# Second attention layer: keys projected for four batches at a time, and the even step's exponentials taken head by head from the score bank

## What is computed

```python
q = (layernorm(x) @ Wq)                # 16 heads of 64
k, v = ctx[:, :77] @ Wk, ctx[:, :77] @ Wv            # 77 text keys
k_ip, v_ip = ctx[:, 77:] @ Wk_ip, ctx[:, 77:] @ Wv_ip   # 51 image keys
out = softmax(q k^T / 8) v + softmax(q k_ip^T / 8) v_ip
x = x + out @ Wo + bo
```

## Time and profile before

| | |
|---|---|
| median of 3 runs | 666.91 us (665.79 to 667.15) |
| profiled execution | 667.46 us, of which the span of instructions is 665.7 us |
| PE busy | 617.7 us (93%) |
| DVE busy | 492.1 us (74%) |
| ACT busy | 461.8 us (69%) |
| POOL busy | 309.8 us (47%) |
| chain that ended last | PE 64%, ACT 11%, issue 9%, POOL 7%, DVE 4%, DMA 3% |

### The profile page before, as it was taken

The page is one execution under the profiler, slowest core; times in us unless marked ns, Lnnn a source line. Parts: engine busy times, 40 slices in busy tenths (PEclk is TensorE's granted clock), DMA queues, the critical chain, the costliest instruction groups (busy, mean ns, idle before and its releaser), DMA issues.

```text
span 665.7 us, 16842 instructions
## 1 busy us (share of the span) xinstructions
PE 617.7 (93%) x5833; PEld 568.2 (85%) x5833; DVE 492.1 (74%) x1370; ACT 461.8 (69%) x1397; POOL 309.8 (47%) x444
## 2 busy tenths in 40 slices
PE   5898999999999999999999999999999987998990
PEld 5787888898888899999989989889888976988990
DVE  6578676586886869888898896888675675674654
ACT  5988999998888986656565656665663545665762
POOL 4365354354434444444444352445336575565550
PEclk9999999999999999999999999999897999998995
DMA  9800000000000000346654060000000001212215
GB/s 226 256 2 1 1 2 1 2 1 3 1 1 1 3 17 2 127 95 126 114 118 91 2 159 1 2 1 1 1 6 28 26 25 47 64 57 65 77 49 198
DMA packets 49612, 33.36 MB, mean 50 GB/s; under 512 B 9508, under 2 KB 46088, under 8 KB 49528
## 3 DMA queue, kind: packets, MB, share of 16 engines
q1 hardware_dynamic: 47256, 27.61, 16.8%
q0 software_dynamic: 2272, 4.67, 2.1%
HBM read 17.64 MB, written 14.63 MB: 48 GB/s over the span
## 4 chain that ended last, share of the span: by engine, by line
PE 64%; ACT 11%; issue 9%; POOL 7%; DVE 4%; DMA 3%; SPq 0%; POOLq 0%; DVEq 0%; ACTq 0%
PE ps_h L812 7%; PE ps_j L590 7%; PE ps_s L759 7%; ACT scores L987 7%; PE ps_t L797 6%; PE ps_h L829 6%; PE ps_j L369 5%; PE ps_j L371 4%; PE ps_j L370 4%; PE ph L1717 4%; PE py L1728 4%; POOL probs L1531 3%; POOL xs_scratch L1642 2%; PE pf L620 2%; PE pf L677 1%
## 5 line engine op out<-in xcount | busy, mean ns | idle before, releaser
L1531 POOL TENSOR_TENSOR probs<-scores,rsums 128x308 f32<-128x308 f32 (+1 forms) x192 | 153.5, 814 | 203.5 <-DVE rsums L1276 203.3
L987 ACT ACTIVATE scores<-scores,neg_max 128x128 f32<-128x128 f32 x256 | 99.8, 398 | 0.1
L956 ACT ACTIVATE probsT<-ps_t 128x512 f32<-128x512 f32 x128 | 76.3, 596 | 20.2 <-PE ps_t L797 19.8
L797 PE MATMUL ps_t<-ident,probs 128*128 128x128 f32 x512 | 78.4, 276 | 7.9 <-ACT probsT L956 4.3
L759 PE MATMUL ps_s<-KT,QT 64*128 64x128 f32 x1024 | 75.7, 288 | 0.8 <-ACT KT L859 0.8
L853 ACT ACTIVATE QT<-ps_j 128x512 f32<-128x512 f32 x64 | 38.1, 596 | 52.4 <-PE ps_j L371 52.4
L812 PE MATMUL ps_h<-probsT,V 128*64 128x128 f32 x1024 | 70.3, 279 | 1.4 <-DVE x_sb L1031 1.4
L759 PEld LDWEIGHTS ps_s<-KT,QT 64*128 64x128 f32 x1024 | 63.3, 190 | 8.7 <-issue 2.4
L829 PE MATMUL ps_h<-Wo,headsT 128*128 128x128 f32 x512 | 67.8, 275 | 1.7 <-ACT headsT L949 1.7
L797 PEld LDWEIGHTS ps_t<-ident,probs 128*128 128x128 f32 x512 | 58.7, 141 | 12.5 <-POOL probs L1531 8.3
L812 PEld LDWEIGHTS ps_h<-probsT,V 128*64 128x64 f32 x1024 | 55.0, 137 | 12.4 <-issue 11.1
(11 more groups left out here) (241 smaller groups left out, 1682.8 us busy)
## 6 DMA issues: line engine op xcount, KB each, us to landing
xs_scratch<-xs SPq DMA_DIRECT2D x8, 1032.0 KB, 7.7
xt<-xs_scratch SPq DMA_DIRECT2D x39, 64.5 KB, 1.8
w1b<-in_L_ffn_w_dram SPq DMA_DIRECT2D x1, 2048.0 KB, 8.2
big_raw<-in_L_ffn_w_dram SPq DMA_DIRECT2D x8, 256.0 KB, 4.8
ysum<-y_scratch SPq DMA_DIRECT2D x4, 512.0 KB, 5.3
Wo<-in_L_xattn_Wo_dram SPq DMA_DIRECT2D x2, 512.0 KB, 4.5
out_dram<-x_sb SPq DMA_DIRECT2D x4, 256.0 KB, 2.4
x_sb<-in_x_dram SPq DMA_DIRECT2D x3, 256.0 KB, 8.8
```

What stands on the lines that cost most here:

```text
L797: ins = nc.tensor.transpose(ps_pT[:, j * S:(j + 1) * S], probs[s % 2][:, j, :], ident[:, :])
L956: nc.scalar.activation(probsT[(s - 2) % 4][:, :, :].rearrange("p h s -> p (h s)"), ps_pT[:, :], ACT.Copy).then_inc(SS["pT_copied"], 1)
L987: ins = nc.scalar.activation(scores[s % 4][:, j, :], scores[s % 4][:, j, :], ACT.Exp, bias=neg_max[:, s % 4, 0, j:j + 1], accum_out=sums[: ...
L1531: ins = nc.gpsimd.tensor_tensor(probs[(s - 1) % 2][:, :, k0:k1], scores[r][:, :, k0:k1], rsums[:, r, i, :].rearrange("p (h a) -> p h a", a ...
```

## The change

Four edits to layer two, none to layer one.

1. **Keys for two groups.** `k_groups` says for which groups a block's keys are projected: for two groups in one go where it can (14 blocks), for one group in 4 blocks, and in the other 14 blocks not at all, because they were projected before. The keys of the later group wait in `KT_next`, which lies in the last 2048 columns of `big_raw`. A matmul has 2 x 154 or 2 x 102 columns in place of 154 or 102. The two tiles of a block now go to two banks, and so queries always take `ps_j1`, and values `ps_j0`; the second tile waits until the queries are copied out.
2. **Copies of the keys.** Where one instruction copied 512 columns, each tile and group is now copied by one of 256 columns: four for two groups, none where nothing was projected.
3. **The even step's exponential.** ScalarE reads the bank, for each head and each span one instruction with the maximum as bias and the sum as a by-product: eight in place of one. VectorE's shift and sums of the even step go away.
4. **The experts' weights.** SyncE loads the first four experts when it did, and the last four once the last scores are computed, since `KT_next` lies where they go.

```diff
@@ (new, in the trunk)
+        def k_groups(m):
+            g, hb = m % (GROUPS * BLOCKS) // BLOCKS, m % BLOCKS
+            if m < GROUPS * BLOCKS or hb < BLOCKS // 2 and g == 0:
+                return [g]
+            if g % 2 == (1 if hb < BLOCKS // 2 else 0):
+                return [g, g + 1] if g + 1 < GROUPS else [g]
+            return []
...
@@ project_k
+                    bank = k_bank(m, t)
+                    if lay == 1 and t == 1:
+                        pe.wait_ge(SS["q_copied"], m + 1)
                     for (k0, k1), w in zip(SEGS[lay], WK[lay]):
...
+                            of = slice(g, g + len(groups))
+                            dst = bank[:, :].rearrange("p (g c) -> p g c", g=2)[:, 0:len(groups), k0 * PAIR:k1 * PAIR]
+                            hi, lo = (c[:, of, k0:k1, :].rearrange("p g s b -> p g (s b)") for c in (ctxT_hi, ctxT_lo))
+                        ins = three_pass(pe, dst, w, cols, hi, lo)
...
@@ project_v
-                pe.wait_ge(SS["q_copied"], m + 1 + (not last))
+                if m < GROUPS * BLOCKS - 1:
+                    pe.wait_ge(SS["q_copied"], m + 2)
+                else:
+                    pe.wait_ge(SS["v_copied"], m)
+                    if not last and k_groups(m + 1):
+                        pe.wait_ge(SS["k_copied"], k_upto(m + 1) + 1)
...
@@ scores of layer two
-                            wait_pos(pe, SS["shifted"], g * STEPS + s)
+                            pe.wait_ge(SS["exp_ready"], n - 1)
+                            wait_pos(pe, SS["shifted"], m - GROUPS * BLOCKS)
...
@@ ScalarE, exponentials
+                    elif par == 0:
+                        act.wait_ge(SS["max_ready"], n + 1)
+                        act.wait_ge(SS["probs_ready"], n - 3)
+                        for j in range(HB):
+                            for i, (k0, k1) in enumerate(SEGS[1]):
+                                ins = nc.scalar.activation(scores[s % 4][:, j, k0:k1],
+                                                           ps_scores[0][:, j * S + k0:j * S + k1], ACT.Exp,
+                                                           bias=neg_max[:, s % 4, i, j:j + 1],
+                                                           accum_out=sums[:, s % 4, i, j:j + 1])
...
@@ VectorE
-                        for par in range(2):
-                            shifted_scores(n + par, s + par)
+                        shifted_scores(n + 1, s + 1)
...
@@ SyncE
+            for part in range(2):
+                if part == 1:
+                    sp.wait_ge(SS["scores_ready"], NG * STEPS)
+                es = slice(part * E // 2, (part + 1) * E // 2)
+                for e in range(es.start, es.stop):
```

More of the change, by code:

```diff
@@ L364, in trunk, with k_upto, q_bank, k_bank @@
             return lambda N: at(NG - 1, N - (NG - 1) * STEPS)
+        def k_groups(m):
[5 more added lines that the diff above has]
+            return []
+        def k_upto(m):
+            return min(m, GROUPS * BLOCKS) + sum(TILES for i in range(GROUPS * BLOCKS, m) if k_groups(i))
+        def q_bank(m):
+            return ps_proj[(3 * (m % BLOCKS) + 1) % 2 if m < GROUPS * BLOCKS else 1]
+        def k_bank(m, t):
+            return ps_proj[(3 * (m % BLOCKS)) % 2 if m < GROUPS * BLOCKS else t]
+        def v_bank(m):
+            return ps_proj[(3 * (m % BLOCKS)) % 2 if m < GROUPS * BLOCKS - 1 else 0]
+        def k_home(m):
+            return KT[m % BLOCKS % 2] if k_groups(m) else KT_next[:, m % BLOCKS, :, :, :]
         def three_pass(pe, psum, w, w_cols, act_hi, act_lo, start=True, stop=True):
@@ L550, in project_q @@
             def project_q(m, g, hb, lay):
-                wait_pos(pe, SS["k_copied"], m)
+                wait_pos(pe, SS["k_copied"], k_upto(m))
+                if lay == 1:
+                    pe.wait_ge(SS["q_copied"], m)
                 if lay == 0:
@@ L555, in project_q @@
                     pe.wait_ge(s_split0_lo, split_of(0, hb))
-                bank = ps_proj[(3 * hb + 1) % 2]
+                bank = q_bank(m)
                 for t in range(TILES):
@@ L563, in project_k @@
             def project_k(m, g, hb, lay):
+                groups = k_groups(m)
+                if not groups:
+                    return
                 wait_pos(pe, SS["v_copied"], m - 1)
@@ L579, in project_v @@
                     pe.wait_ge(SS["ctx_staged"], G + 1)
-                pe.wait_ge(SS["q_copied"], m + 1 + (not last))
+                if m < GROUPS * BLOCKS - 1:
+                    pe.wait_ge(SS["q_copied"], m + 2)
+                else:
+                    pe.wait_ge(SS["v_copied"], m)
+                    if not last and k_groups(m + 1):
+                        pe.wait_ge(SS["k_copied"], k_upto(m + 1) + 1)
                 if G == 0:
                     pe.wait_ge(s_split0_lo, split_of(2, hb))
-                bank = ps_proj[(3 * hb) % 2]
+                bank = v_bank(m)
                 cols = slice(hb * HB * HD, (hb + 1) * HB * HD)
@@ L759, in step @@
                                     ins = nc.tensor.matmul(ps_scores[half][:, j * S:(j + 1) * S],
-                                                           QT[hb % 2][rows, t, bb, :], KT[hb % 2][rows, t, bb, :],
+                                                           QT[hb % 2][rows, t, bb, :], k_home(m)[rows, t, bb, :],
                                                            start=True, stop=True)
@@ L853, in copy_q @@
                 nc.scalar.activation(QT[hb % 2][:, :, :, :].rearrange("p t b s -> p (t b s)"),
-                                     ps_proj[(3 * hb + 1) % 2][:, :], ACT.Copy,
+                                     q_bank(m)[:, :], ACT.Copy,
                                      scale=float(HD) ** -0.5).then_inc(SS["q_copied"], 1)
             def copy_k(m, hb):
-                act.wait_ge(SS["k_ready"], m + 1)
-                nc.scalar.activation(KT[hb % 2][:, :, :, :],
-                                     ps_proj[(3 * hb) % 2][:, :].rearrange("p (t s b) -> p t b s", t=TILES, b=PAIR),
-                                     ACT.Copy).then_inc(SS["k_copied"], 1)
+                if m < GROUPS * BLOCKS:
+                    act.wait_ge(SS["k_ready"], m + 1)
+                    nc.scalar.activation(KT[hb % 2][:, :, :, :],
+                                         k_bank(m, 0)[:, :].rearrange("p (t s b) -> p t b s", t=TILES, b=PAIR),
+                                         ACT.Copy).then_inc(SS["k_copied"], 1)
+                    return
+                homes = [KT[hb % 2], KT_next[:, hb, :, :, :]][0:len(k_groups(m))]
+                for t in range(TILES if homes else 0):
+                    act.wait_ge(SS["k_ready"], k_upto(m) + t + 1)
+                    for i, home in enumerate(homes):
+                        ins = nc.scalar.activation(
+                            home[:, t, :, :],
+                            k_bank(m, t)[:, i * PAIR * S:(i + 1) * PAIR * S].rearrange("p (s b) -> p b s", b=PAIR),
+                            ACT.Copy)
+                    ins.then_inc(SS["k_copied"], 1)
             def mean_square(g, which, src, name):
@@ L1262, in exp_sums @@
             def exp_sums(n, p4, lay):
-                if lay == 0:
+                if lay == 0 or p4 % 2 == 0:
                     return
@@ L1990, in _ @@
             sp.wait_ge(s_splitm, 2 * RW_GROUPS)
-            for e in range(E):
-                sp.dma_start(w2b[:, e, 0:KT_HID * D].rearrange("p (k n) -> p k n", k=KT_HID),
-                             w2[e, :, :].rearrange("(k p) n -> p k n", p=P)).then_inc(s_w2, 16)
-            sp.dma_start(w2b[:, :, KT_HID * D:W2_COLS],
-                         b2.rearrange("(a e) n -> a e n", a=1).broadcast_to([P, E, D])).then_inc(s_w2, 16)
+            for part in range(2):
[3 more added lines that the diff above has]
+                for e in range(es.start, es.stop):
+                    sp.dma_start(w2b[:, e, 0:KT_HID * D].rearrange("p (k n) -> p k n", k=KT_HID),
+                                 w2[e, :, :].rearrange("(k p) n -> p k n", p=P)).then_inc(s_w2, 16)
+                sp.dma_start(w2b[:, es, KT_HID * D:W2_COLS],
+                             b2[es, :].rearrange("(a e) n -> a e n", a=1).broadcast_to([P, E // 2, D])).then_inc(s_w2, 16)
             def load_tile(i):
```

28 lines of the change are left out of this document (17 added, 11 removed).

## The result

The changed kernel took 679.86 us (median of 4 runs, 679.10 to 681.30), the kernel before 666.58 beside it: 13.3 us slower, ratio 1.0182, 95% interval 1.015 to 1.0214. In a second set of runs the same pair gave 674.25 and 665.04 us, ratio 1.014 (1.0118 to 1.0163). The ratios of this text are those on record, each with its interval; they differ from the quotient of the two medians by up to 0.002 (here 1.0199). The forecast was 669.9 us, range 661 to 677: the sign was right, and the size was off by 6 to 10 us.

What follows compares the result with a forecast made beforehand. The prediction took TensorE as layer two's bound, busy 289.9 of 292.4 us. Its terms, -17.8 + 3.2 + 2.1 + 0.7 + 13.5 + 0.8 + 0.5 = +3.0 us, gave 669.9 us against the median, range 661 to 677.

Steps and rivals of the forecast that it cites:

- keys not projected: TensorE, 14 blocks of layer two: 1.27 us of key matmuls less in each, 17.8 us less, all on the chain.
- double keys, their wait, copies: Blocks projecting for two groups: wider matmuls +3.2 us, second tile's wait and restart +2.1; key copies +0.7.
- exponentials, on the kernel before: ScalarE's eight exponentials: stalls 13.5 us, late maxima 0.8, turns of `xs` 0.5.
- experts' weights: Late load of the last experts' weights: at worst 0.3 us, counted as nothing.
- the first conclusion of its argument: Layer two: TensorE, busy 289.9 of 292.4 us, is the bound, with VectorE's 237.8 us beside it.
- Keys for one group cost what they did: The 4 blocks projecting keys for one group: no extra cost.
- The delay: ScalarE, even step: eight exponentials take 2.4 us against 0.53, so the heads' copy comes 1.84 us later.
- the twelve whose slack of 1.9 us or more costs nothing: Twelve blocks where feed-forward or router matmuls stand ahead of the output projection: no stall from the late heads' copy.
- Rival A: ScalarE: accumulator reads hide or bank is cheaper; delay 1.1 to 1.4 us, time 658.5 to 661.7; chance 0.22.
- Rival C: TensorE: wide key matmuls are dearer as the groups' columns lie apart; +5.9 us, 675.8; chance 0.06.
- Rival D: TensorE: more idle time costs clock near the router; +2 us, 672; upper edge of the forecast, which has 0.45.

Runs made afterwards that it cites:

- keys left out: The kernel before without the key matmuls and copies of 14 blocks of layer two, scores using stale keys: ratio 0.9916, 5.6 us less.
- keys alone: The changed kernel with the even step's exponential undone (edits 1, 2 and 4 without edit 3), against the kernel before: ratio 1.0007, 669.10 us.
- exponentials alone: The kernel before with only edit 3, the even step's eight exponentials: ratio 1.0252, 16.8 us on 668.63.

## Why the prediction was wrong

| term | forecast | measured |
|---|---|---|
| keys not projected | -17.8 | -5.6 (-7.5 to -3.6), keys left out |
| double keys, their wait, copies | +6.0 | +6.1, keys alone (1.0007) less keys left out (0.9916) |
| exponentials, on the kernel before | +14.8 | +16.8, exponentials alone (1.0252) |
| exponentials, on top of the keys | +14.8 | +8.9 (1.014 less 1.0007) to +11.7 (with 1.0182) |
| experts' weights | 0 | none seen |

- **The step that failed** is the first conclusion of its argument, "So a matmul taken away shortens the layer, and work taken from VectorE by itself gives nothing", and with it the term of 17.8 us. It was read from the mean over 292 us, in which VectorE has 55 us to spare. Over blocks 14 to 17 it had 2.7. Seven of the first twelve blocks without keys ran into waits for VectorE or GpSimd, which did not exist before: these blocks gave 8.6 of 15.2 us. Block 30, the thirteenth, ran into the router's `hidT` and a lower clock. Both halves of the sentence fall: with the keys reduced, work taken from VectorE did give something. Block 8 took 8.64 us with keys alone and 7.49 with the exponentials changed too, block 17 took 8.60 and 7.64, and putting VectorE's sums back cost 1.8 us in the blocks without keys. That fits edit 3 costing 16.8 us by itself and less on top of the keys (13.9 and 9.2 to 9.8 us in blocks 1 to 25). This smaller cost hid 3 to 6 us of the 12 us by which the keys fell short, so the sum missed by less than its largest term did.
- **Double keys were right.** In keys alone each of the twelve blocks 2 to 5, 10 to 13 and 18 to 21 grew by 0.37 to 0.40 us (forecast 0.38). That the whole row of the table comes out at 6.1 is in part luck: it is a difference of two ratios whose intervals are about 2 us each way. "Keys for one group cost what they did" was wrong: block 1's second tile waited 0.42 us for the queries' copy and the block grew by 0.66: six matmuls of one group, 0.1 us each, don't cover a copy of 0.6 us that starts only when the queries are done.
- **The delay was right**, 1.79 us against 1.84, and so, roughly, was its price. There were 16 waits, 0.20 to 0.75 us each, 7.8 in all, where 17 of 10.3 in all were forecast; by themselves the exponentials made those 16 blocks 11.8 us longer, more than the waits show. Blocks 26 and 28 grew by 2.35 and by 1.6 to 2.7 us (forecast 2.13 with double keys, and 1.4). Missed was block 18, where the copies of the biases stood behind the eight exponentials, and the transposes waited for them by 1.1 us: 1.3 us. The prediction had this block among the twelve whose slack of 1.9 us or more costs nothing, and looked there at the projection and not at the transposes.
- **Rival A's arithmetic was right**, its condition was not met. It said that a delay of 1.1 us would leave 2.1 us of stalls in place of 13.5, 11.4 less; without the reads, at a delay of 1.05 us, it was 12.5 us less (0.9953 against 1.014). The reads did not hide: each moved the next exponential by 0.09 us. The Trainium skill, ScalarE: Activation LUTs, section What ACT_TABLE_LOAD costs, gives 280 ns + 0.833 ns an element less 93 ns of overlap, by which an estimate for the eight is 1.92 us. They took 1.58 without reads and 2.32 with. For a single instruction the trace agrees with the page: 0.35 and 0.33 us for 77 and 51 columns, 0.34 and 0.32 as an estimate by the page. The overlap differs: neighbours without reads overlapped by 0.14 us. And the page has no price for the read, which by these numbers is 0.09 us.
- **Rival C** fell with the double keys. **Rival D**, a fall of the clock, came true in part: block 30 had a granted clock of 0.86 in both profiles of the change and took 1.4 and 1.0 us more than before where 1.27 less was forecast. The kernel before has such stretches too (0.87 and 0.80 in blocks 27 and 29 of its first profile, only 0.89 in block 29 of its second), which makes 3 us between two profiles of one kernel.
- VectorE lost 35 us of busy time, not 50.

## What to carry to other kernels

A bound read as a mean over a stage is not a bound in each block: before counting a saving, take the busy time of the second engine over just the blocks in which the work goes away, and cap the saving by its spare time. The cap was too high here as well (11.6 us against 8.6), so follow the second engine's chain through one such block too. An instruction that gives a sum "for free" is not free where its engine stands ahead of the critical one: price its accumulator read, and put what others wait for ahead of it or between. Two edits that unload different engines should be measured apart and together, since each decides what the other is worth.

## What the hardware showed that was not expected

- An accumulator read behind an ACTIVATE of 51 to 77 columns costs 0.09 us of ScalarE's time, a third of the pair (0.29 against 0.20 us).
- The experts' phase, the same instructions in the same order, took 106.4 to 113.4 us in the profiles, 111.7 and 107.5 for one program. The cause stays open.
- Leaving out 1.3 us of matmuls brought the lower clock into block 30, in eight of eleven profiles, and never with the matmuls there (seven). It came behind waits of TensorE of 0.7 to 1.6 us, and behind the same wait of 0.73 us it came in two profiles and stayed away in two (in one more it stayed away behind 1.19 us), so the wait alone doesn't decide it. Three pairs of kernels that differ only in the keys of the router's blocks show it each time; what besides the wait decides was not tested.
